# The opening of a perceiver layer: values over eight PSUM banks, row norms in pairs on two engines, keys projected ahead of queries

## The chip, the cores and the metric

The kernel runs on one core of one Trainium2 chip. A core has five engines with instruction streams of their own: TensorE (PE, matrix products into PSUM), VectorE (DVE), ScalarE (ACT), GpSimd (POOL) and SyncE (SP), which here only issues DMAs. They meet in semaphores. The metric is the device time of one execution in microseconds, the median of several runs.

## What is computed

One layer of three residual blocks over 512 rows of 1024 columns, in float32:

```python
x = x + cross_attention(layernorm(x), ctx)     # 16 heads of 64, causal
x = x + bitlinear_ffn(layernorm(x))            # weights rounded to -1, 0, 1, rows to int8
x = x + moe(layernorm(x))                      # 8 experts, top 2, and a shared one
# in the cross attention:
qp = q @ Wq.T                                  # q = layernorm(x): 512 x 1024
k, v = split(latent_kv @ Wkv_expand.T)         # latent_kv: 8192 x 256, of which the causal mask leaves 512 rows
out = softmax(mask(qh @ kh.T / 8)) @ vh
```

The change lies in the first 40 us: everything up to the exponentials of the first pair of heads. What follows is the same code.

## The kernel before

**Exact products.** To keep float32, each operand is split into a high part (a copy in a format that TensorE takes in full) and a low part (operand less high part), and `three` (L287) issues three matmuls for one product: high by high, high by low, low by high. So every operand needs a copy (as a rule ScalarE's) and a subtraction (VectorE's or GpSimd's).

**Loads.** SP issues in program order: the context `CTX` (two k-tiles of 128 by 512), the value weights in `RA[0]` (two k-tiles of 1024 columns, L387 and L388), the four tiles of rows `XRES`; then `qk_load(0)`, the query and key weights of head pair 0 (640 KB), also into `RA[0]` once `free_a[0]` says that it is read; four chunks of later weights into `RA[1]` to `RA[4]`; two more into `RX`; then `qk_load(1)` (L396), which waits until GpSimd has split the first. The chunks are only summed here (mean of absolute values, `absum` and `absum_x`); they share out between ScalarE (L1187, L1230) and VectorE (L684, L678).

**Values.** `values(n)` computes one 128 by 512 tile of V of four row tiles by two column halves, n = 2t + q, six matmuls each: for both k-tiles three. They go round four banks, `VB = (6, 7, 0, 1)`, so from the fifth on each waits for the evacuation of the one four before (`v_evac`, L1164). The first waits for both low parts of k-tile 0.

**Row norms.** `layer_norm_stats` (VectorE) takes the statistics of all four tiles (L359, L361), adds the constant, and waits for ScalarE's square root (`root`, L348), which stands in ScalarE's program behind four evacuations. `inv_sqrt` (L324 to L328) refines the reciprocal in five tiny instructions, each waiting for the one before; a sixth gives the offset. Four instructions (L667) write the normalised rows `XN`.

**Transposes.** `x_rows(t)` transposes a row tile in two halves through banks 2 to 5, ScalarE evacuates the high part (`xt_evac`, L1170), VectorE the low part (L672). Tiles 2 and 3 wait for the banks of 0 and 1. Two value tiles stand between them in TensorE's order.

**GpSimd** waits for all four `XN` and then splits the weights of pair 0 (`w_split`, L583 and L587, in two parts of 768 and 512 columns, high and low each).

**Projection.** `project_first(0)` takes the first half of the query product into bank 6 (12 matmuls), then the keys into bank 7 (6), `project_rest(0)` the other 12; `k_split` and `q_split` on ScalarE and VectorE split keys and queries; `scores`, row maxima (L702), exponentials (L1214) follow. From pair 1 on a loop does the same, with the attention of the pair before in between.

Of the kernel before, what the change touches and what calls it, by code (L numbers as in the profile page):

```python
# [21 lines left out]
P = 128  # L22
TOK, DM, LAT = 512, 1024, 256
NT = TOK // P
# [18 lines left out]
VB = (6, 7, 0, 1)  # L43
# [27 lines left out]
def program(nc, x, ctxT, wv, wqk, wo, wbit, n_gate, n_down, n_rms, wrt, wmoe, out, rows_dram):  # L71
    es = ExitStack()
    with es:
# [182 lines left out]
        for n in ("const", "v_eps", "sqrt", "ln",  # L256
                  "x_in0", "x_in1", "x_in2", "x_in3", "ctx_in", "norm_in",
                  "xn", "xt_pe", "xt_hi", "xt_lo", "ct_hi", "ct_lo", "wv_hi", "wv_lo", "v_pe", "v_ev", "wv_in",
# [93 lines left out]
        def layer_norm_stats(e):  # L352

            o = own["dve"]
            for t in range(NT):
                if veps[0] == 0:
                    e.wait_ge(s(f"x_in{t}"), 16)
                for h in range(2):
                    ins = e.bn_stats(BN[:, t, h, :], XRES[:, t, h * 512:h * 512 + 512])  # L359
                o(ins)  # L360
                o(e.bn_aggr(MV[:, t, :], BN[:, t, :, :].rearrange("p a b -> p (a b)")))  # L361
            e.tensor_scalar(col(2), MV[:, :, 1:2].rearrange("p a b -> p (a b)"), 1e-5, None, ALU.add)\
                .then_inc(s("v_eps"), 1)
            veps[0] += 1
            e.wait_ge(s("v_eps"), veps[0])
            inv_sqrt(e, col(2), col(3), col(0), veps[0])
            e.scalar_tensor_tensor(out=col(1), in0=MV[:, :, 0:1].rearrange("p a b -> p (a b)"), scalar=-1.0,
                                   in1=col(0), op0=ALU.mult, op1=ALU.mult).then_inc(s("ln"), 1)
# [182 lines left out]
        def _(e):  # L551
# [22 lines left out]
            def w_split(c, first, second=False):  # L574
                for q, at in enumerate((slice(0, WQA * P), slice(WQA * P, STRIP))):
# [4 lines left out]
                    if not first:  # L580
                        e.wait_ge(s(("k_pe", "q_pe")[q]), c)
# [13 lines left out]
            e.wait_ge(s("xn"), NT)  # L595
# [57 lines left out]
        def _(e):  # L653
# [3 lines left out]
            e.wait_ge(s("ct_hi"), 1)  # L657
            e.tensor_tensor(CTL[:, :, :], CTX[:, :, :], CTH[:, :, :].bitcast(f32), ALU.subtract)\
                .then_inc(s("ct_lo"), 1)
            for k in range(KL):  # L660
                e.wait_ge(s("wv_hi"), k + 1)
                e.tensor_tensor(WVL[:, k, :], RA[0][:, k * DM:k * DM + DM], WVH[:, k, :].bitcast(f32), ALU.subtract)\
                    .then_inc((s("wv_lo"), free_a[0])[k], 1)
            layer_norm_stats(e)
            e.wait_ge(s("ln"), 1)
            for t in range(NT):
                e.tensor_scalar(XN[t][:, :], XRES[:, t, :], col(0)[:, t:t + 1], col(1)[:, t:t + 1], ALU.mult, ALU.add)\  # L667
                    .then_inc(s("xn"), 1)
            for n in range(2 * NT):
                t, q = divmod(n, 2)  # L670
                e.wait_ge(s("xt_hi"), n + 1)
                e.tensor_tensor(XTL[:, 4 * q:4 * q + 4, t * P:t * P + P], r3(bank[2 + n % 4], 4),  # L672
                                XTH[:, 4 * q:4 * q + 4, t * P:t * P + P].bitcast(f32), ALU.subtract)\
                    .then_inc(s("xt_lo"), 1)
# [478 lines left out]
        def _(e):  # L1153
            e.preload_act_table(ACT.Sqrt)
            e.wait_ge(s("ctx_in"), 16)
# [17 lines left out]
            for n in range(4):  # L1173
                v_evac(n)
# [754 lines left out]
```

## Time and profile before

| | us |
|---|---|
| median of 3 runs | 683.06 (681.15 to 683.9) |
| profiled execution | 681.58 |
| its span | 680.0 |
| PE busy | 632.8 (93%) |
| DVE busy | 490.5 (72%) |
| ACT busy | 410.8 (60%) |
| POOL busy | 144.6 (21%) |
| mean granted TensorE clock | 0.987 of full |

The span runs from the first to the last instruction; 1.58 us lie around it. Matmuls are pipelined and each row's duration includes the way through the array, so a busy TensorE is not one at its peak: the distance between the starts of two rows tells the rate. In the page's chain that ended last TensorE has 61%, VectorE and ScalarE 15% each, and 6% is time in which an engine waited for nothing that the profile shows. In a timeline, "[1.99 <-issue]" behind a row is the idle time before it and what ended it. "(x36)" in a view by windows counts instructions.

### The profile page before, as it was taken

How to read it: one execution, taken by the hardware profiler on the slowest of the kernel's cores; microseconds unless marked ns; L12 is line 12 of the kernel's file. 1: busy time of each engine (PE TensorE's matmuls, PEld its weight loads, DVE VectorE, ACT ScalarE, POOL GpSimd, SP SyncE). 2: the span in 40 equal slices, each digit the busy share in tenths (PEclk: the TensorE clock that was granted, in tenths of full speed). 3: DMA queues.
4: the chain of work that ended last, by engine and by line, in shares of the span. 5: the costliest groups of instructions: out<-in, count | busy, mean ns of one | idle time of the engine just before them, and what ended most of it. 6: DMA issues, size and time to landing. Idle time of an engine off the chain costs nothing.

```text
span 680.0 us, 9662 instructions
## 1 busy us (share of the span) xinstructions
PE 632.8 (93%) x3275; PEld 475.9 (70%) x3289; DVE 490.5 (72%) x790; ACT 410.8 (60%) x531; POOL 144.6 (21%) x140
## 2 busy tenths in 40 slices
PE   4899999998999999749999999999999999999993
PEld 3778888886885444324467878787888778788772
DVE  5788887888786898688898366829192884564877
ACT  3778888888648898672574165527171771634740
POOL 1373445415000344219400400000000000000041
PEclk9999999999999999969999999999999999999997
DMA  8967776755167878709975619937466598292957
GB/s 332 384 241 294 300 291 240 314 236 192 52 278 282 337 293 357 302 0 363 409 294 232 267 67 380 406 137 301 173 238 256 193 380 349 104 362 70 387 174 265
DMA packets 30969, 179.02 MB, mean 263 GB/s; under 512 B 3808, under 2 KB 3808, under 8 KB 14688
## 3 DMA queue, kind: packets, MB, share of 16 engines
q1 hardware_dynamic: 25920, 161.39, 61.2%
q0 software_dynamic: 5024, 17.30, 6.7%
q8 instruction: 14, 0.23, 0.1%
q14 instruction: 11, 0.09, 0.0%
HBM read 155.62 MB, written 23.07 MB: 263 GB/s over the span
## 4 chain that ended last, share of the span: by engine, by line
PE 61%; DVE 15%; ACT 15%; issue 6%; DMA 2%; DVEq 0%; POOL 0%; ACTq 0%; SPq 0%
PE BK L293 13%; PE BK L299 13%; PE BK L294 13%; PE BK L287 9%; ACT PR L1214 4%; PE BK L1591 3%; ACT RA L1187 2%; PE BK L1691 2%; PE BK L1813 2%; DMA RD<-wbit 2%; PE BK L1576 1%; DVE BH L836 1%; ACT RA L1284 1%; PE BK L1745 1%; DVE HE L963 1%
## 5 line engine op out<-in xcount | busy, mean ns | idle before, releaser
L293 PE MATMUL BK<-WH,ETH 128*128 128x512 f32 x272 | 107.4, 395 | 1.5 <-ACT ETH L1435 1.4
L294 PE MATMUL BK<-WL,ETH 128*128 128x512 f32 x272 | 106.1, 390 | 0.0
L949 DVE TENSOR_TENSOR WL<-RA,WH 128x2048 fp32r<-128x2048 f32 x40 | 89.4, 2287 | 9.7 <-ACT WH L1402 9.5
L1402 ACT ACTIVATE WH<-RA 128x2048 fp32r<-128x2048 f32 x40 | 73.8, 1924 | 2.3 <-PE BK L1691 2.3
L1461 ACT ACTIVATE HTH<-BK 128x256 fp32r<-128x256 f32 x32 | 11.4, 383 | 95.2 <-PE BK L1813 95.1
L299 PE MATMUL BK<-WH,ETL 128*128 128x512 f32 x272 | 67.4, 390 | 0.0
L293 PEld LDWEIGHTS BK<-WH,ETH 128*128 128x128 f32 x272 | 51.0, 188 | 16.1 <-DVE WL L949 3.4
L647 POOL DMA_INDIRECT GA<-rows,SLOT x4 | 4.9, 1230 | 269.7 <-DVE WL L949 268.8
L299 PEld LDWEIGHTS BK<-WH,ETL 128*128 128x128 f32 x272 | 51.0, 188 | 10.6
L294 PEld LDWEIGHTS BK<-WL,ETH 128*128 128x128 f32 x272 | 51.1, 188 | 10.2
L963 DVE TENSOR_TENSOR HE<-BK,SI 128x256 f32<-128x256 f32 x34 | 12.9, 420 | 58.9 <-PE BK L299 58.1
L615 POOL TENSOR_TENSOR HB<-HB,ND (+2 forms) x28 | 31.1, 1127 | 111.5 <-DVE BH L836 110.7
L293 PE MATMUL BK<-WH,HTH 128*128 128x512 f32 x128 | 51.3, 401 | 0.6 <-ACT HTH L1461 0.6
L294 PE MATMUL BK<-WL,HTH 128*128 128x512 f32 x128 | 50.0, 391 | 0.0
L1284 ACT ACTIVATE RA<-RA,RT 128x2048 int16<-128x2048 f32 x22 | 43.8, 2001 | 5.3 <-DVE RT L765 3.1
L949 DVE TENSOR_TENSOR WL<-RC,WH 128x2048 fp32r<-128x2048 f32 x20 | 45.0, 2286 | 0.7 <-ACT WH L1402 0.7
L1645 PE MATMUL BK<-TG,XQ 128*128 128x512 bf16 x188 | 42.1, 379 | 0.3
L1402 ACT ACTIVATE WH<-RC 128x2048 fp32r<-128x2048 f32 x20 | 37.3, 1920 | 4.6 <-PE BK L299 4.6
L583 POOL TENSOR_TENSOR WQH<-RA,ONEF 128x768 fp32r<-128x768 f32 (+1 forms) x16 | 25.2, 1572 | 64.9 <-DMA RA<-wqk 46.5
L1691 PE MATMUL BK<-TD,HQT 128*128 128x512 bf16 x171 | 38.5, 381 | 0.3
L1214 ACT ACTIVATE PR<-BK,RT 128x512 f32<-128x512 f32 (+1 forms) x64 | 32.8, 536 | 7.6 <-DVE RT L702 7.4
L1187 ACT ACTIVATE RA<-RA 128x2048 f32<-128x2048 f32 x19 | 36.2, 1915 | 0.0
(252 smaller groups left out, 1400.5 us busy)
## 6 DMA issues: line engine op xcount, KB each, us to landing
RA<-wbit SPq DMA_DIRECT2D x53, 1024.0 KB, 6.5
RA<-wmoe SPq DMA_DIRECT2D x40, 1024.0 KB, 6.8
RC<-wmoe SPq DMA_DIRECT2D x20, 1024.0 KB, 7.7
rows<-ZERO POOLq DMA_DIRECT2D x34, 256.0 KB, 12.2
XG<-rows SPq DMA_DIRECT2D x15, 512.0 KB, 7.1
RD<-wbit SPq DMA_DIRECT2D x7, 1024.0 KB, 6.3
rows<-YS SPq DMA_DIRECT2D x14, 512.0 KB, 6.7
RA<-wqk SPq DMA_DIRECT2D x8, 640.0 KB, 7.4
```

The source lines that it names most:

```text
L287: m = e.matmul(dst, st, mv, start=first and i == 0 and j == 0, stop=last and i == n - 1 and j == 2)
L293: e.matmul(dst, sh, mh, start=first and i == 0, stop=False)
L294: e.matmul(dst, sh, ml, start=False, stop=False)
L299: m = e.matmul(dst, sl, mh, start=False, stop=i == len(pairs) - 1)
L615: e.tensor_tensor(HB[:, t, cs], HB[:, t, cs], ND[:, cs], ALU.mult).then_inc(s("hnd"), 1)
L949: e.tensor_tensor(WL[m][:, q * RAW:q * RAW + RAW], RC[j][:, :], WH[m][:, q * RAW:q * RAW + RAW].bitcast(f32), ALU.subtract)\
L1187: e.activation(RA[j][:, :], RA[j][:, :], ACT.Abs, accum_out=ACCW[:, column]).then_inc(free_a[j], 1)
L1214: ins = e.activation(PR[h][:, off:off + P * (i + 1)], STR[h][:, off:off + P * (i + 1)], ACT.Exp, bias=NM[:, h, i:i + 1], accum_out=RS[:, h ...
L1284: e.activation(RB16[j], RB[j][:, :], ACT.Copy, scale=SW[:, 0:1]).then_inc(s("rnd"), 1)
L1402: e.activation(WH[m][:, q * RAW:q * RAW + RAW], RC[2 * m + q][:, :], ACT.Copy)\
L1645: m = e.matmul(bank[out], XQ[:, k, t * P:t * P + P], weights[:, k, :], start=k == 0, stop=k == KD - 1)
L1691: m = e.matmul(bank[2 * (t % 2) + q], HQT[t % 2][:, k, :], (TD1[:, k, :] if k < 16 else TD2[:, k - 16, :])[:, q * 512:q * 512 + 512], star ...
```

## The change

- The context is loaded, copied and subtracted by k-tile: two DMAs, the second behind the first half of the value weights (five waits for DMAs in place of four). The value weights are copied by column half, the second k-tile's right half first.
- TensorE starts with k-tile 0 alone (`values_first`): for one column half the high by high products of all four row tiles, then low by high, then high by low. Each kind waits only for what it reads. The eight results lie in all eight banks. `values_rest` adds k-tile 1, right half first. No value matmul waits for an evacuation any more; the transposes wait for the four of the right half (banks 2 to 5).
- The low parts of the second k-tile of the value weights are made by GpSimd, which also frees `RA[0]`. GpSimd no longer waits for `XN`.
- Norms by pairs: statistics of tiles 0 and 1, constant, statistics of 2, scale of the pair, tile 0 normalised, statistics of 3, the second pair's. ScalarE normalises tiles 1 and 3 and takes two square roots, the first behind three evacuations, the second behind six. All low parts of transposed rows stand behind tile 2 on VectorE.
- TensorE transposes all four tiles behind the values; the keys of pair 0 are projected before the queries, and no longer wait for the transposed rows. GpSimd's split of pair 1 waits for `wq_pe`, the first half of the queries.
- `qk_load(1)` is issued ahead of the two loads into `RX`. Of the absolute sums one on ScalarE (`RX[0]`) and one on VectorE (`RX[1]`) stand behind the query split in place of ahead of it, and the key split comes earlier.

```diff
@@ sync
-            e.dma_start(CTX[:, :, :], ctxT).then_inc(s("ctx_in"), 16)
+            e.dma_start(CTX[:, 0, :], ctxT[:, 0, :]).then_inc(s("ctx_in"), 16)
             e.dma_start(RA[0][:, 0:DM], wv[:, 0:DM]).then_inc(s("wv_in"), 16)
+            e.dma_start(CTX[:, 1, :], ctxT[:, 1, :]).then_inc(s("ctx_in2"), 16)
...
+            qk_load(1)
             for j in range(2):
                 e.dma_start(RX[j][:, :], wbit[8 + j]).then_inc(in_x[j], 16)
-            qk_load(1)
@@ gpsimd
-            e.wait_ge(s("xn"), NT)
+            for n, q in enumerate((1, 0)):
+                cs = slice(q * 512, q * 512 + 512)
+                e.wait_ge(s("wv_hi"), n + 3)
+                e.wait_ge(s("wv_lo"), 2)
+                e.tensor_tensor(WVL[:, 1, cs], RA[0][:, DM + q * 512:DM + q * 512 + 512], WVH[:, 1, cs].bitcast(f32),
+                                ALU.subtract).then_inc((s("wv_lp"), free_a[0])[n], 1)
             w_split(0, True)
@@ vector
-            layer_norm_stats(e)
-            e.wait_ge(s("ln"), 1)
-            for t in range(NT):
+            def row_norm(t):
+                e.wait_ge(s("ln"), t // 2 + 1)
                 e.tensor_scalar(XN[t][:, :], XRES[:, t, :], col(0)[:, t:t + 1], col(1)[:, t:t + 1], ALU.mult, ALU.add)\
                     .then_inc(s("xn"), 1)
...
+            row_stats(e, 0)
+            row_stats(e, 1)
+            row_variance(e, 0)
+            row_stats(e, 2)
+            row_scale(e, 0)
+            row_norm(0)
+            row_stats(e, 3)
+            row_variance(e, 2)
+            row_scale(e, 2)
+            row_norm(2)
+            rows_t_lo(0)
+            rows_t_lo(1)
+            rows_t_lo(2)
+            rows_t_lo(3)
...
             absum(2, slice(5, 6), 16)
+            k_split(0)
             absum(4, slice(7, 8), 16)
-            k_split(0)
+            q_split(0)
             absum_x(1, 9)
-            q_split(0)
@@ scalar
-            for n in range(4):
+            for n in range(3):
                 v_evac(n)
-            root(e, col(2), col(3))
+            root(e, col(2)[:, 0:2], col(3)[:, 0:2])
+            v_evac(3)
+            row_norm(1)
             v_evac(4)
             v_evac(5)
-            xt_evac(0)
-            xt_evac(1)
+            root(e, col(2)[:, 2:4], col(3)[:, 2:4])
             v_evac(6)
             v_evac(7)
+            xt_evac(0)
+            row_norm(3)
+            xt_evac(1)
             xt_evac(2)
             xt_evac(3)
...
+            k_split(0)
             absum(1, slice(4, 5), 16)
             absum(3, slice(6, 7), 16)
+            q_split(0)
             e.wait_ge(in_x[0], 16)
             e.activation(RX[0][:, :], RX[0][:, :], ACT.Abs, accum_out=ACCW[:, 8:9]).then_inc(sum_x[0], 1)
-            k_split(0)
-            q_split(0)
@@ tensor
+            def values_first(q):
+                cs = slice(q * 512, q * 512 + 512)
+                for n, (A, B) in enumerate(((CTH, WVH), (CTL, WVH), (CTH, WVL))):
+                    e.wait_ge(*((s("wv_hi"), q + 1), (s("ct_lo"), 1), (s("wv_lo"), q + 1))[n])
+                    for t in range(NT):
+                        e.matmul(bank[VB[q][t]], A[:, 0, t * P:t * P + P], B[:, 0, cs], start=n == 0, stop=False)
...
-            for n in range(6):
-                values(n)
-            e.wait_ge(s("const"), 15)
-            x_rows(0)
-            x_rows(1)
-            values(6)
-            values(7)
-            x_rows(2)
-            x_rows(3)
+            values_first(0)
+            values_first(1)
+            e.wait_ge(s("ct_lo"), 2)
+            e.wait_ge(s("wv_lp"), 1)
+            values_rest(1)
+            e.wait_ge(free_a[0], 1)
+            values_rest(0)
+            e.wait_ge(s("const"), 15)
+            e.wait_ge(s("v_ev"), NT)
+            for t in range(NT):
+                x_rows(t)
             e.wait_ge(s("v_ev"), 2 * NT)
-            e.wait_ge(s("xt_lo"), 2 * NT)
...
+                if isinstance(c, int) and c == 0:
+                    three(e, bank[7], part(range(KL), CTH, CTL, 4), True, True).then_inc(s("k_pe"), 1)
+                    e.wait_ge(s("xt_lo"), 2 * NT)
+                m = three(e, bank[6], part(range(4), XTH, XTL, 0), True, False)
```

## Rows read from the trace of the kernel before

**Rows 1.** Stages: from:to, length, busy PE PEld DVE ACT POOL, clock, DMA, GB/s
```profile
9.50:20.00 10.50, 10.47 (x36) 8.04 (x36) 8.92 (x21) 3.08 (x6) 0.00 (x0) 1.00 1.01 415
```

**Rows 2.** Timeline of ScalarE's opening: start, length, line, operation, out<-in
```profile
7.06 1.06 ACT L1159 ACTIVATE WVH<-RA 128x1024 fp32r<-128x1024 f32 x1 [1.89 <-DMA RA<-wv]
17.80 0.20 ACT L348 ACTIVATE SM<-SM 128x4 f32<-128x4 f32 x1
```

**Rows 3.** Timeline of TensorE, the first and the tenth matmul
```profile
9.52 0.76 PE L287 MATMUL BK<-WVH,CTH 128*128 128x512 f32 x1 [9.52 <-DVE WVL L662]
13.49 0.59 PE L287 MATMUL BK<-WVH,CTH 128*128 128x512 f32 x1
```

**Rows 4.** Timeline of TensorE, first and last of the 30 matmuls of projection 0
```profile
28.71 0.47 PE L287 MATMUL BK<-XTH,WQH 128*128 128x512 f32 x1 [1.99 <-issue]
35.37 0.39 PE L287 MATMUL BK<-XTH,WQL 128*128 128x512 f32 x1
```

**Rows 5.** Timeline of VectorE: statistics, root, normalised rows, low parts
```profile
15.27 1.29 DVE L359 BATCH_NORM_STATS2 BN<-XRES 128x6 f32<-128x512 f32 x2
18.10 0.18 DVE L324 RECIPROCAL SM<-SM 128x4 f32<-128x4 f32 x1 [1.09 <-ACT SM L348]
19.31 2.98 DVE L667 TENSOR_SCALAR XN<-XRES,SM 128x1024 f32<-128x1024 f32 x4
26.12 2.48 DVE L672 TENSOR_TENSOR XTL<-BK,XTH 128x512 fp32r<-128x512 f32 x4 [1.44 <-ACT XTH L1170]
```

**Rows 6.** Timeline of VectorE and ScalarE, end of the opening
```profile
34.35 2.28 DVE L678 TENSOR_REDUCE ACCW<-RX 128x1 f32<-128x2048 f32 x1
36.54 0.68 DVE L693 SCALAR_TENSOR_TENSOR QL<-BK,QH 128x512 fp32r<-128x512 f32 x1
31.19 1.94 ACT L1230 ACTIVATE RX<-RX 128x2048 f32<-128x2048 f32 x1
35.79 0.60 ACT L1203 ACTIVATE QH<-BK 128x512 fp32r<-128x512 f32 x1 [2.08 <-PE BK L287]
36.92 1.28 ACT L1235 ACT_TABLE_LOAD   x1
39.01 0.69 ACT L1214 ACTIVATE PR<-BK,RT 128x512 f32<-128x512 f32 x1 [0.81 <-DVE RT L702]
```

**Rows 7.** SP issue and landing of query weights, GpSimd split
```profile
10.70 0.33 SPq L396 DMA_DIRECT2D RA<-wqk  x1
RA<-wqk SPq DMA_DIRECT2D x1, 640.0 KB, 4.3
22.38 1.86 POOL L583 TENSOR_TENSOR WQH<-RA,ONEF 128x768 fp32r<-128x768 f32 x1 [18.40 <-DVE XN L667]
24.31 1.83 POOL L587 TENSOR_TENSOR WQL<-RA,WQH 128x768 fp32r<-128x768 f32 x1
27.46 1.28 POOL L587 TENSOR_TENSOR WQL<-RA,WQH 128x512 fp32r<-128x512 f32 x1
```

**Rows 8.** Timeline of VectorE alone and beside GpSimd
```profile
149.51 2.29 DVE L731 TENSOR_TENSOR WOL<-RA,WOH 128x2048 fp32r<-128x2048 f32 x1 [1.11 <-ACT WOH L1240]
151.36 4.88 POOL L605 TENSOR_TENSOR WOL<-RA,WOH 128x2048 fp32r<-128x2048 f32 x1 [14.03 <-ACT WOH L1240]
155.58 0.17 DVE L710 RECIPROCAL RT<-RT 128x4 f32<-128x4 f32 x1
160.13 4.61 POOL L605 TENSOR_TENSOR WOL<-RA,WOH 128x2048 fp32r<-128x2048 f32 x1
163.72 3.17 DVE L731 TENSOR_TENSOR WOL<-RA,WOH 128x2048 fp32r<-128x2048 f32 x1
```

**Rows 9.** Timeline of GpSimd and VectorE where both have work queued
```profile
240.28 1.71 POOL L615 TENSOR_TENSOR HB<-HB,ND  x1
240.79 1.76 DVE L808 TENSOR_SCALAR TX<-RA 128x2048 bf16<-128x2048 int16 x1
```

**Rows 10.** Busy time by stage, the columns of rows 1, behind the last matmul
```profile
670.00:675.00 5.00, 0.00 (x0) 0.00 (x0) 4.89 (x6) 0.00 (x0) 0.00 (x0) 0.77 0.62 254
```

More of the change, by code:

```diff
@@ L350, in program, with row_stats, row_variance, row_scale @@
         veps = [0]
-        def layer_norm_stats(e):
+        def row_stats(e, t):
             o = own["dve"]
-            for t in range(NT):
[L356 to L362, printed above, removed]
+            e.wait_ge(s(f"x_in{t}"), 16)
+            for h in range(2):
+                ins = e.bn_stats(BN[:, t, h, :], XRES[:, t, h * 512:h * 512 + 512])
+            o(ins)
+            o(e.bn_aggr(MV[:, t, :], BN[:, t, :, :].rearrange("p a b -> p (a b)")))
+        def row_variance(e, t):
+            e.tensor_scalar(col(2)[:, t:t + 2], MV[:, t:t + 2, 1:2].rearrange("p a b -> p (a b)"), 1e-5, None, ALU.add)\
                 .then_inc(s("v_eps"), 1)
             veps[0] += 1
[L365 to L368, printed above, removed]
+        def row_scale(e, t):
+            two = slice(t, t + 2)
+            inv_sqrt(e, col(2)[:, two], col(3)[:, two], col(0)[:, two], veps[0])
+            e.scalar_tensor_tensor(out=col(1)[:, two], in0=MV[:, two, 0:1].rearrange("p a b -> p (a b)"), scalar=-1.0,
+                                   in1=col(0)[:, two], op0=ALU.mult, op1=ALU.mult).then_inc(s("ln"), 1)
         def tile_stats(e, t, eps):
@@ L580, in w_split @@
                     if not first:
-                        e.wait_ge(s(("k_pe", "q_pe")[q]), c)
+                        e.wait_ge(s(("wq_pe" if second else "k_pe", "q_pe")[q]), c)
                     hi, lo = (T[:, :, :].rearrange("p a b -> p (a b)")[:, at] for T in (WQH, WQL))
@@ L656, in _ @@
             e.sem_inc(s("h"), 8)
[L657 to L663, printed above, removed]
-            layer_norm_stats(e)
@@ L667, in _, with rows_t_lo @@
+            context_lo(1)
+            def row_norm(t):
+                e.wait_ge(s("ln"), t // 2 + 1)
                 e.tensor_scalar(XN[t][:, :], XRES[:, t, :], col(0)[:, t:t + 1], col(1)[:, t:t + 1], ALU.mult, ALU.add)\
                     .then_inc(s("xn"), 1)
[L669 to L674, printed above, removed]
+            def rows_t_lo(t):
+                for q in range(2):
+                    n = 2 * t + q
+                    e.wait_ge(s("xt_hi"), n + 1)
+                    e.tensor_tensor(XTL[:, 4 * q:4 * q + 4, t * P:t * P + P], r3(bank[2 + n % 4], 4),
+                                    XTH[:, 4 * q:4 * q + 4, t * P:t * P + P].bitcast(f32), ALU.subtract)\
+                        .then_inc(s("xt_lo"), 1)
@@ L1542, in project_first @@
                 e.wait_ge(s("wq_a"), c + 1)
-                three(e, bank[6], part(range(4), XTH, XTL, 0), True, False)
-                e.wait_ge(s("ot_lo"), c if not isinstance(c, int) or c else 1)
+                if isinstance(c, int) and c == 0:
+                    three(e, bank[7], part(range(KL), CTH, CTL, 4), True, True).then_inc(s("k_pe"), 1)
+                    e.wait_ge(s("xt_lo"), 2 * NT)
+                m = three(e, bank[6], part(range(4), XTH, XTL, 0), True, False)
+                if isinstance(c, int) and c == 0:
+                    m.then_inc(s("wq_pe"), 1)
+                    return
+                e.wait_ge(s("ot_lo"), c)
                 three(e, bank[7], part(range(KL), CTH, CTL, 4), True, True).then_inc(s("k_pe"), 1)
```

66 lines of the change are left out of this document (40 added, 26 removed).

## The prediction

> **What bounds the kernel now.** I read the page first, whose chain that ended last is mostly TensorE's; but that is an average over stages, and the change touches nothing behind the first head pair. So next came the busy time by stages: from 9.5 to 20 TensorE is busy for 10.47 of 10.50 us, and the DMA engines are full at 415 GB/s [rows 1]. Both are misleading, which only the third view shows, the timeline of the opening engine by engine: the chain passes from engine to engine, and these are its stations. ScalarE's high part of the first value weights starts when the DMA lands at 7.06 [rows 2]; TensorE begins at 9.52 [rows 3], because VectorE makes the low part first. Its first ten matmuls are 0.44 us apart, which for 512 columns is the 1.2 GHz level (the granted clock of that stretch stands at 1.00 in [rows 1], so here the steps tell it), and the later ones 0.23 (28.71 to 35.37 is 29 steps [rows 4]), the 2.4 GHz level; before 9.52 it had done nothing. The square root of the row norms is at 17.80, since ScalarE takes it behind four evacuations [rows 2]; VectorE starts on it at 18.10, normalises from 19.31 to 22.29 and ends the low parts of the transposed rows at 28.60 [rows 5]. Then thirty projection matmuls run from 28.71 to 35.76 [rows 4]. The low queries start at 36.54, behind the last 2.28 us reduction, and the exponentials, after the first row maxima, at 39.01 [rows 6]. That last number is what I carry: from it on both kernels do the same work in the same order, pair after pair, with nothing I can find that would give time back.
>
> **The change, part by part, in order of time.**
>
> *First matmul.* Ahead of the value weights lies half a context (262 KB less, 0.63 us at 415 GB/s [rows 1]), so they land near 6.4 (bounds 5.9 to 7.06, if the smaller pieces bring nothing). The first high part is half as wide: the row of 1.06 for 1024 columns [rows 2] and 0.60 for 512 [rows 6] say 0.6. No low part is needed for the first four matmuls. TensorE starts near 7.1, 2.4 us early. The context splits lie in the waits for DMAs and cost nothing; if the DMAs came no earlier they would still be ahead of the weights.
>
> *Values.* Still 48 matmuls. Ten at 0.44 last to 11.5. The third finished bank is now the 33rd matmul (24 first parts, 3 for each bank), 22 steps of 0.23 later: it ends at 16.9. Before, the fourth bank ended at 17.3. So of the 2.4 us only 0.4 reach the square root: ScalarE evacuates the third bank (0.5) and takes the root at 17.4; VectorE has it at 17.7. The statistics of rows 0 to 2 (1.3 a tile and the aggregate, 15.27 [rows 5]) are done by 14.5 and wait.
>
> *GpSimd.* It now makes the low parts of the second value weights, 1.28 each of 512 columns [rows 7], 9.0 to 11.6, and these free the weight buffer; so the SP queue, which waits for it, issues the first query weights at 11.6 and not 10.70 [rows 7]. These landed 4.3 us after issue [rows 7]; with the older rows drained by then I take 15.5 (15.0 to 15.9). Before, GpSimd waited for the four normalisations and split them from 22.38 to 28.74, 6.36 us [rows 7]. That wait is gone: it splits from 15.5 to about 22. Nobody needs the result before the projection.
>
> *The collision.* Now the split lies upon the row norms. What rows show: a subtraction of VectorE with two SBUF inputs took 2.29 alone and 3.17 from 163.72 on, while GpSimd was busy until 164.74; a reciprocal took 0.17 in the middle of a GpSimd instruction [rows 8]. And where GpSimd has instructions queued the two alternate: GpSimd's row from 240.28 is 1.71 long and ends at 241.99, VectorE's from 240.79 ends 0.56 behind that [rows 9]. So an instruction of VectorE waits for the whole of GpSimd's, gets its turn, and its successor waits for the whole of GpSimd's next. Behind the root stand a reciprocal, three tensor-tensor forms, one scalar form, and one combination that reads two SBUF operands, all on two columns and each waiting for the one before (0.2 a step, 18.10 to 19.31 [rows 5]). No row shows such tiny instructions beside GpSimd, so their cost lies between nothing and one GpSimd instruction each. I take the full wait, because the rows above are blocked to the end of GpSimd's instruction whatever their own length. Then: multiplication asked at 17.9, granted at 19.3 (1.86 and 1.83 of split gone [rows 7]); the next behind the third instruction at 20.7; the next behind the fourth at 22.15; the norm's scale is ready at 22.7, against 18.9 without the collision. The Trainium skill has a rule for this (SBUF — State Buffer, section "Who interferes with whom"): a VectorE instruction with two SBUF inputs, or in a two-port mode, and a GpSimd instruction that reads SBUF exclude each other for the whole instruction. The trace agrees for large ones, 3.17 against 2.29; it states no exception for small ones.
>
> *Second pair of rows.* Row 0 is normalised at 23.5 (0.75 each [rows 5]), the statistics of row 3 follow to 25.1, ScalarE meanwhile does row 1 (1.06) and two evacuations, root at 25.25, scale ready at 26.7, row 2 at 27.5. The low parts of the transposed rows now wait behind all this. ScalarE puts its own row 3 (1.06) ahead of the second row's evacuations, so these low parts run without a gap only from the third on: 29.1 + 6 × 0.62 = 32.85 (0.62 each [rows 5]), against 28.60. Taking two of the four normalisations from VectorE (1.5 us) is paid with a second root and a second chain of six (1.5).
>
> *Projection.* The six key matmuls now run in the wait, 30.9 to 32.3; 24 instead of 30 lie behind the rows, which brings 1.4. Queries end at 32.9 + 23 × 0.23 + 0.39 = 38.6 (35.76 before).
>
> *Absolute sums.* One of VectorE (2.28) and one of ScalarE (1.9) move behind the query splits. They are no longer in front of anything that is late, but they are in front of the row maxima and of the table load. High queries at 38.6, low at 39.2, maxima at 42.0; ScalarE: 38.6 + 0.5 + 1.9 + 0.6 + 1.28 = 42.9 [rows 6]. Exponentials start at 42.9 and not 39.01: +3.9. Their data: the two loads now stand behind the second query weights, issued at 22; with four loads of 1 MB issued from 12 on and 0.65 MB ahead of them, at 415 GB/s they land by 32, needed at 39.
>
> *Clock.* TensorE ends the values at 20.3 and waits for row 0 until 23.5. The level held through 1.99 us of idleness at 28.7 [rows 4], and near the end, in a stretch without a matmul from 670 on, the granted clock has a mean of 0.77 over five microseconds, so it stood at 1 for some 2.7 and at half for the rest [rows 10]. So 3.2 us may lose it. Keys and the first queries then run at 0.44: 0 to 1.4 us. I take 0.6.
>
> Sum: +3.9 + 0.6 = +4.5. On the profiled execution's own 681.58 that is 686.1. It lies 1.5 below the median of 683.06, to which I apply the same difference: 687.6.
>
> **Rivals.**
> *Small instructions are not blocked* (not slower). The scale is then ready at 18.9; only the normalisation of row 0 waits 0.5 for GpSimd. Low parts end near 29.5, queries at 35.2 (0.6 early, for the keys are out of the way), low queries at 35.8, maxima at 38.6, ScalarE 35.2 + 4.3 = 39.5. With the moved sums that is +0.5: 683.5, range 682 to 685. It decides at the first tiny instruction behind the root. For it: the reciprocal of [rows 8]. Against it: that one reads a single operand.
> *The clock falls and stays down* through keys and queries: 30 × 0.21 = 6.3 at most, of which the keys hide some; with the collision +9, 691 to 692. Against it: at the start ten matmuls brought the clock up [rows 3].
> *The opening simply works*: weights at 5.9, no blocking, the root not late. Then the queries end at 34.3, exponentials near 38.4: 682.4. It can't be more, since the maxima stand behind three reductions and two splits of VectorE (7.9 us) after the last low part, wherever they are put.
> *The identity function of the row norms needs another table than the root*: 1.28 [rows 6] each way, 2.6 to 5 us more. The copies around the root reloaded nothing, so I hold it small, inside the upper range. The Trainium skill says (ScalarE: Activation LUTs, "Table sets: the hidden batching unit") that identity is in every set; by it the cost is nothing, and no row here shows the function.
>
> **How the numbers follow.** Collision with the clock kept or lost briefly 0.54 (685.9 to 689.5); small instructions free 0.34; opening works 0.04; clock down or tables 0.08. A measurement of this kernel can tell about 0.5%, 3.4 us, from no change; the boundary of slower is 686.5. Of the first case 0.44 lies above it, of the last all: slower 0.52, same 0.45, faster 0.03. Range 682.6 to 690.5, leaving out a tenth on each side. The likeliest case's own is 685.9 to 689.5.
>
> **What would show it.** VectorE's small rows near 17.9 to 22 of over 1 us each (right) or 0.16 (the rival). First matmul near 7.1; root near 17.4; GpSimd's split from 15.5; last low part near 32.9 (rival 29.5); key matmuls wholly before it; a spacing of 0.44 in keys and queries if the clock fell; first exponential at 42.9 against 39.5; and the distance from it to the end as before, 641.0. The prediction is wrong if the query weights land after the norms are done, for then nothing collides, or if the later stages take the delay back.

## The result and the profile after

The changed kernel takes 686.51 us (median of 7 runs, 684.64 to 688.14) beside 683.44 for the kernel before on the same chip (7 runs, 681.15 to 684.4). The ratio is 1.005, with a 95% interval of 1.0032 to 1.0068, so it is slower by 2.2 to 4.6 us. The profiled execution took 686.51, with a span of 684.8 and a mean clock of 0.982 (681.58, 680.0 and 0.987 before).

These are the stations of the opening, in us from the span's start. The second column is read or worked out from the rows ahead of the prediction, the last from the rows below.

| station | before | forecast | after |
|---|---|---|---|
| first matmul | 9.52 | 7.1 | 6.53 |
| first query weights issued | 10.70 | 11.6 | 12.86 |
| GpSimd's split begins | 22.38 | 15.5 | 18.11 |
| (first) root | 17.80 | 17.4 | 17.46 |
| row 0: normalisation asked | 19.31 | 22.7 | 23.10 |
| row 0 normalised | 20.1 | 23.5 | 24.94 |
| second root | none | 25.25 | 26.62 |
| last low part of the transposed rows ends | 28.60 | 32.85 | 34.10 |
| first exponential | 39.01 | 42.9 | 44.25 |
| from it to the end of the span | 641.0 | 641.0 | 640.55 |

**Where the time goes** is in VectorE's timeline of the changed kernel (start, length, then as in [rows 5]). The six tiny instructions behind the root stand one below the other; in the kernel before they took 0.2 a step from 18.10 to 19.31.

```profile
17.76 0.17 DVE L324 RECIPROCAL SM<-SM 128x2 f32<-128x2 f32 x1 [2.03 <-ACT SM L348]
17.95 0.16 DVE L325 TENSOR_TENSOR SM<-SM 128x2 f32<-128x2 f32 x1
18.15 1.82 DVE L326 TENSOR_TENSOR SM<-SM 128x2 f32<-128x2 f32 x1
20.00 0.17 DVE L327 TENSOR_SCALAR SM<-SM 128x2 f32<-128x2 f32 x1
20.20 1.64 DVE L328 TENSOR_TENSOR SM<-SM 128x2 f32<-128x2 f32 x1
21.88 1.18 DVE L371 SCALAR_TENSOR_TENSOR SM<-MV,SM 128x2 f32<-128x2 f32 x1
23.10 1.84 DVE L681 TENSOR_SCALAR XN<-XRES,SM 128x1024 f32<-128x1024 f32 x1
...
28.05 0.81 DVE L681 TENSOR_SCALAR XN<-XRES,SM 128x1024 f32<-128x1024 f32 x1
...
30.42 3.68 DVE L688 TENSOR_TENSOR XTL<-BK,XTH 128x512 fp32r<-128x512 f32 x6 [0.36 <-ACT XTH L1215]
```

And GpSimd's timeline of the same stretch:

```profile
10.31 2.52 POOL L604 TENSOR_TENSOR WVL<-RA,WVH 128x512 fp32r<-128x512 f32 x2 [6.34 <-ACT WVH L1192]
18.11 1.83 POOL L588 TENSOR_TENSOR WQH<-RA,ONEF 128x768 fp32r<-128x768 f32 x1 [5.28 <-DMA RA<-wqk]
20.02 1.80 POOL L592 TENSOR_TENSOR WQL<-RA,WQH 128x768 fp32r<-128x768 f32 x1
21.79 1.25 POOL L588 TENSOR_TENSOR WQH<-RA,ONEF 128x512 fp32r<-128x512 f32 x1
23.13 1.27 POOL L592 TENSOR_TENSOR WQL<-RA,WQH 128x512 fp32r<-128x512 f32 x1
```

Add start and length on both sides. VectorE's tiny row from 18.15 ends at 19.97, GpSimd's from 18.11 at 19.94. VectorE's from 20.20 ends at 21.84, GpSimd's from 20.02 at 21.82; VectorE's from 21.88 at 23.06, GpSimd's from 21.79 at 23.04. Three times an instruction on two columns ends 0.02 or 0.03 behind the GpSimd instruction during which it was asked. The row from 17.95 was asked before GpSimd had begun and took 0.16. The three cost 1.66, 1.48 and 1.02 us above their own length, 4.2 together. The normalisation of row 0 (0.81 alone, at 28.05) took 1.84, 1.0 more, and ended 0.54 behind GpSimd's fourth.

The second chain of six, 26.86 to 28.01, took 0.2 a step. GpSimd was done by then.

How the split came to lie there: SP's issue in the timeline, the transfer in the view of DMAs from 12 to 20 (size, us to landing), and ScalarE's timeline.

```profile
12.86 0.33 SPq L401 DMA_DIRECT2D RA<-wqk  x1
```

```profile
RA<-wqk SPq DMA_DIRECT2D x1, 640.0 KB, 5.2
```

```profile
5.85 1.15 ACT L1192 ACTIVATE WVH<-RA 128x512 fp32r<-128x512 f32 x2 [1.53 <-DMA RA<-wv]
...
9.60 1.15 ACT L1192 ACTIVATE WVH<-RA 128x512 fp32r<-128x512 f32 x2 [1.19 <-DMA RA<-wv]
...
17.46 0.20 ACT L348 ACTIVATE SM<-SM 128x2 f32<-128x2 f32 x1
...
26.62 0.20 ACT L348 ACTIVATE SM<-SM 128x2 f32<-128x2 f32 x1 [1.31 <-DVE SM L363]
...
42.96 1.28 ACT L1284 ACT_TABLE_LOAD   x1
44.25 0.69 ACT L1263 ACTIVATE PR<-BK,RT 128x512 f32<-128x512 f32 x1
```

The second k-tile of the value weights was there at 9.60, so GpSimd's low parts ended at 12.83. The query weights were issued at once and landed at 18.1, 0.3 behind the start of VectorE's chain. This moment is not fixed: in the eight traces with these opening loads (this one and e1, e3 to e6, e8, e9, below) the query weights were issued between 11.83 and 13.21 and landed between 15.4 (e9) and 18.4 (e5).

**TensorE** of the changed kernel: its first matmuls, the first transposes, and the key product; then the busy time by stage (columns of [rows 1]).

```profile
6.53 2.08 PE L1555 MATMUL BK<-WVH,CTH 128*128 128x512 f32 x4 [6.53 <-ACT WVH L1192]
...
25.09 3.65 PE L1570 MATMUL BK<-IDF,XN 128*128 128x128 f32 x16 [4.76 <-DVE XN L681]
...
32.18 0.48 PE L287 MATMUL BK<-CTH,WQH 128*128 128x512 f32 x1
32.49 0.39 PE L287 MATMUL BK<-CTL,WQH 128*128 128x512 f32 x1
32.72 0.39 PE L287 MATMUL BK<-CTH,WQL 128*128 128x512 f32 x1
```

```profile
20.00:24.00 4.00, 0.33 (x2) 0.00 (x0) 3.90 (x4) 0.90 (x1) 3.90 (x3) 0.80 1.01 426
24.00:28.00 4.00, 2.91 (x14) 2.94 (x15) 3.49 (x11) 2.69 (x7) 0.40 (x1) 0.50 0.99 386
...
32.00:36.00 4.00, 3.66 (x18) 2.74 (x17) 4.00 (x5) 3.20 (x4) 0.00 (x0) 1.00 0.19 74
```

It started 3.0 us earlier than before, finished the values and then stood for 4.76 us. The granted clock fell to 0.50, and the transposes ran at the lower level. By the keys it was back (steps of 0.23).

### The profile page after: what moved, and what is told of

Same layout as the page of the kernel before. It is cut to its first block, busy times and chain, and to the rows that moved or that the text cites. A ratio compares the mean times of both kernels' runs of the same rounds, so it can differ in the third digit from the quotient of the medians.

```text
span 684.8 us, 9676 instructions
## 1 busy us (share of the span) xinstructions
PE 635.9 (93%) x3275; PEld 477.7 (70%) x3289; DVE 494.3 (72%) x796; ACT 413.4 (60%) x537; POOL 147.1 (21%) x142
## 3 DMA queue, kind: packets, MB, share of 16 engines
q0 software_dynamic: 5024, 17.30, 6.6%
## 4 chain that ended last, share of the span: by engine, by line
PE 61%; DVE 15%; ACT 15%; issue 4%; DMA 3%; DVEq 0%; POOL 0%; SPq 0%; ACTq 0%
PE BK L293 14%; PE BK L294 13%; PE BK L299 13%; PE BK L287 8%; ACT PR L1263 5%; ACT RA L1236 3%; PE BK L1646 2%; PE BK L1746 2%; PE BK L1868 2%; PE BK L1631 1%; DMA RA<-wbit 1%; PE BK L1555 1%; DVE BH L866 1%; ACT RA L1333 1%; ACT PTH L1270 1%
```

## The experiments

The theory: GpSimd's split lies on the norms' chain of tiny instructions, and each of these waits for a whole GpSimd instruction. The rivals: the late root and the two chains are the cost, or the moved sums are, or the load order, or the clock. All experiments were run beside the kernel before; its median was 683.18 for e1 to e4, 683.33 for e5 to e9, 682.84 for e10 and e11.

**e1: the split waits for VectorE's two normalisations again.**

```diff
+            e.wait_ge(s("xn"), 2)
             w_split(0, True)
             w_split(1, False, True)
```

> The changed kernel, but GpSimd again waits before its split of pair 0, now for the two tiles that VectorE normalises. Theory of the collision: the instructions of 1.82, 1.64, 1.18 and 1.84 us behind the first root fall to 0.16 and 0.8, the scale of the first pair is ready near 19 in place of 23.1, the last low part of the transposed rows ends near 29 in place of 34.1, and the first exponential starts at 39.5 to 40.5 in place of 44.25 (the two loads for the moved sums now come later, near 37, and may cost the rest); time about 4 us under the changed kernel, level with the kernel before within 0.3%. Rival, the order of VectorE's own work (a second root, a second chain of tiny instructions, all low parts behind tile 2) is what costs: the tiny instructions get short, but the first exponential stays at 42 or later and the time over 685.

Measured: 685.9, ratio 1.0041 (1.0024 to 1.0057). The timelines of e1, VectorE and TensorE, and one stage:

```profile
17.89 0.16 DVE L326 TENSOR_TENSOR SM<-SM 128x2 f32<-128x2 f32 x1
...
18.68 0.81 DVE L682 TENSOR_SCALAR XN<-XRES,SM 128x1024 f32<-128x1024 f32 x1
...
38.70 2.29 DVE L709 TENSOR_REDUCE ACCW<-RX 128x1 f32<-128x2048 f32 x1 [2.38 <-DMA RX<-wbit]
```

```profile
45.62 4.00 PE L1632 MATMUL BK<-IDF,PR 128*128 128x128 f32 x20 [2.74 <-DVE PR L745]
```

```profile
46.00:48.00 2.00, 2.00 (x11) 2.00 (x10) 1.88 (x6) 0.29 (x1) 0.00 (x0) 0.50 0.99 401
```

The chain is free: every tiny row has its 0.16 or 0.17, row 0 is asked at 18.68 and not 23.10, and the last low part ends at 29.10 and not 34.10. So the collision is there and the split causes it. But of these 5.0 us only 2.6 reach the first exponential (41.62), and almost nothing the median: 685.9 is what the rival asked for, while the rows are those of the theory. The row from 38.70 says why: a sum waits 2.38 us for its DMA. The change had also put `qk_load(1)` ahead of the two `RX` loads in SP's queue. `qk_load(1)` waits for GpSimd's split, which now ends near 30; it is issued at 29.85 and `RX` at 30.22 (24.42 and 24.79 in the changed kernel, where nothing waited for them). The maxima stand behind that sum. In addition TensorE stood for 2.74 us ahead of the transposes of the first pair's probabilities, the clock fell to 0.50, and the distance from the first pair's exponentials to the second pair's was 17.4 instead of 16.5.

**e2: the kernel before, with the wait of GpSimd for `XN` removed.**

```diff
-            e.wait_ge(s("xn"), NT)
             w_split(0, True)
```

> The kernel before, with only GpSimd's wait for the four normalised tiles taken out, so that it splits as soon as the weights have landed (near 15). Theory of the collision: three or four of the tiny instructions behind the root take 1.2 to 1.8 us, the first tile is normalised near 22 in place of 19.3, the first exponential starts near 41.4 in place of 39.0, time +2.4 us (+0.35%). Rival, that the two engines do not exclude each other for tiny operands and the long rows of the changed kernel are waits for something else: nothing moves, within 0.1%.

Measured: 687.36, ratio 1.0066 (1.0043 to 1.009): one removed line makes the old kernel slower, by the ratio 4.5 us (2.9 to 6.1). GpSimd, VectorE and TensorE of e2:

```profile
17.16 1.85 POOL L587 TENSOR_TENSOR WQL<-RA,WQH 128x768 fp32r<-128x768 f32 x1
18.96 1.29 POOL L583 TENSOR_TENSOR WQH<-RA,ONEF 128x512 fp32r<-128x512 f32 x1
20.33 1.27 POOL L587 TENSOR_TENSOR WQL<-RA,WQH 128x512 fp32r<-128x512 f32 x1
```

```profile
19.06 1.22 DVE L326 TENSOR_TENSOR SM<-SM 128x4 f32<-128x4 f32 x1
...
20.51 1.10 DVE L328 TENSOR_TENSOR SM<-SM 128x4 f32<-128x4 f32 x1
...
21.85 2.98 DVE L666 TENSOR_SCALAR XN<-XRES,SM 128x1024 f32<-128x1024 f32 x4
```

```profile
31.27 0.46 PE L287 MATMUL BK<-XTH,WQH 128*128 128x512 f32 x1 [1.99 <-issue]
...
31.93 0.63 PE L287 MATMUL BK<-XTH,WQL 128*128 128x512 f32 x1
```

The two blocked rows end at 20.28 and 21.61, 0.03 and 0.01 behind GpSimd's. The query weights landed earlier here, at 15.2, so less of the split lies on the chain. A third row, from 18.73, took 0.30 and ends at 19.03, 0.02 behind GpSimd's. The normalisation is asked 2.5 us late (21.85 against 19.31), 2.1 of it the chain and 0.4 a later root. That is the delay that I expected, though I had expected three or four rows over 1 us. But the first exponential is 4.15 late, at 43.16, not 2.4. The other 1.6 are the clock: the same 1.99 us of idleness as in [rows 4] ended this time in steps of 0.43 (31.93, 32.35, 32.78 and on to 34.49), and only from 34.91 on in 0.23. I had not expected that.

**e3: the changed kernel with the sums in their old places, ahead of the query splits.**

```diff
 (VectorE)
-            q_split(0)
             absum_x(1, 9)
+            q_split(0)
 (ScalarE)
-            q_split(0)
             e.wait_ge(in_x[0], 16)
             e.activation(RX[0][:, :], RX[0][:, :], ACT.Abs, ...)
+            q_split(0)
```

> The changed kernel, but with the two absolute sums ahead of the query split again on ScalarE and on VectorE. Theory of the prediction (the sums behind the split stand in front of the first exponential, the time ahead of it is idle on both engines by 1.5 and 1.7 us): ScalarE's high queries 0.3 later, VectorE's low queries 0.7 later, first exponential 0.5 earlier, at 43.7; time -0.5 us, which can be read in the trace and not in the medians. Rival, that the sums in front delay the scores by their full length: first exponential at 45 or later.

Measured: 686.34, ratio 1.0046 (1.003 to 1.0063), the same as the changed kernel. The first exponential is at 43.52, 0.73 sooner. The norms were 0.46 earlier by themselves (row 0 was asked at 22.64), but the last sixteen transposes still ran at the lower clock level (0.50 from 28 to 32, against 0.84), and by the end of the last low part only 0.14 of that lead was left (33.96 against 34.10). So 0.59 comes from the place of the sums, where I had expected 0.5; e4 and e8 below give the same. VectorE's chain of e3, however, shows a form that the changed kernel didn't show blocked:

```profile
18.04 1.25 DVE L325 TENSOR_TENSOR SM<-SM 128x2 f32<-128x2 f32 x1
...
19.52 1.68 DVE L327 TENSOR_SCALAR SM<-SM 128x2 f32<-128x2 f32 x1
```

The instruction with one tensor operand (L327) waits too, and which of the six are caught differs from one execution to the next.

**e8 and e4: the wait and the old order of loads; and with the sums ahead as well.** e8 is e1 with this, e4 is e8 with the edit of e3.

```diff
-            qk_load(1)
             for j in range(2):
                 e.dma_start(RX[j][:, :], wbit[8 + j]).then_inc(in_x[j], 16)
+            qk_load(1)
```

> The changed kernel with GpSimd's wait and with the two loads for the moved sums ahead of the second query weights, but the two sums still behind the query split. It stands between the run with the wait alone (first exponential 41.6, which waited 2.4 us for such a load) and the one with all three (38.1). Theory: the load costs 2.2 of these 3.5, the sums' place 1.2: first exponential at 39.3 to 39.5. Rivals: 38.1 (the place of the sums costs nothing) or 41.6 (the load was not it). No clock lost in the first pair's transposes, so that pair's period is 16.7 and not 17.4; time 1.2 us over the run with all three.

> The changed kernel with GpSimd's wait, the two sums ahead of the query split, and their two loads ahead of the second query weights: what is left of the change is the values over eight banks, the norms by pairs and the keys ahead of the queries. Theory: last low part near 29, last query matmul near 34.9 (35.76 before), low queries near 36.9, first exponential at 38.7 (39.0 before); time within 0.2% of the kernel before, some 4.5 us under the changed one. Rival, that the order of the norms costs by itself: first exponential at 40.5 or later.

Measured: e8 682.7, ratio 0.9983 (0.9966 to 1.0001); e4 682.34, 0.9987 (0.9971 to 1.0002). ScalarE's first exponential of e8, and of e4:

```profile
38.77 0.69 ACT L1264 ACTIVATE PR<-BK,RT 128x512 f32<-128x512 f32 x1
```

```profile
38.12 0.69 ACT L1264 ACTIVATE PR<-BK,RT 128x512 f32<-128x512 f32 x1 [0.86 <-DVE RT L733]
```

This is the main finding. With the collision and what hangs on it gone, the changed kernel's first exponential moves from 44.25 to 38.77, and by the ratios it gains 0.67%, 4.6 us. What is left of the change in e8 stands 0.24 ahead of the kernel before at this station and is not to be told from it by time. (In e4 VectorE took the low queries at 35.65, where I had expected 36.9, since the sum ahead of them began sooner.) Against e1, the order of the loads is worth 2.85 there, once the split is late (expected: 2.2). The sums behind the splits cost 0.65 at the first exponential (expected: 1.2) and 0.4 at the second pair's, and nothing that the times show.

One interval sorts the runs better than the single station. From the end of the last low part to the first exponential it is 10.41 in the kernel before, 10.15 where VectorE's sum stands behind the query split (the changed kernel, e5, e8, e11) and 9.56 or 9.57 where it stands ahead (e3, e4, e9, e10). Only where something else came in between was it longer: the late load in e1, the clock in e2, both in e6. So the place of the sum costs 0.59 each time, and everything ahead of the last low part passes through to the first exponential one for one. At that part e8 and e4 stand at 28.62 and 28.55, the kernel before at 28.60 (29.18 and 28.88 in e10 and e11, with the same code up to it): TensorE's start, 3 us earlier, and the norms by pairs have together brought at most 0.6 there.

**e5: the root ahead of the first evacuations, no wait.** In the changed kernel the variance of rows 0 and 1 is ready at 14.30, and ScalarE takes the root at 17.46, behind three evacuations.

```diff
-            for n in range(3):
-                v_evac(n)
             root(e, col(2)[:, 0:2], col(3)[:, 0:2])
-            v_evac(3)
+            for n in range(4):
+                v_evac(n)
```

> The changed kernel with ScalarE's first square root ahead of the evacuations instead of behind three of them; no wait of GpSimd's added. Theory (ports, and a root that is late although its input is ready at 14.3): the scale of the first pair is ready near 17.1, before GpSimd's split begins at 17.5 to 18, tile 0 is normalised near 17.9; now the second chain lies beside the split and has the rows of over 1 us, so the last low part ends near 31 in place of 34.1 and the first exponential is at 41 to 41.5 in place of 44.25; time 2 to 3 us under the changed kernel. Rival (only the first chain matters, the second is short): first exponential at 39.5.

Measured: 684.63, ratio 1.001 (0.9997 to 1.0022). The first chain now runs before the split, 16.12 to 17.30. The second falls into it; GpSimd's four rows start at 18.52, 20.43, 22.20 and 23.54. VectorE of e5:

```profile
19.59 0.79 DVE L363 TENSOR_SCALAR SM<-MV 128x2 f32<-128x2 f32 x1
...
20.85 1.40 DVE L325 TENSOR_TENSOR SM<-SM 128x2 f32<-128x2 f32 x1
22.29 1.19 DVE L326 TENSOR_TENSOR SM<-SM 128x2 f32<-128x2 f32 x1
...
23.71 1.10 DVE L328 TENSOR_TENSOR SM<-SM 128x2 f32<-128x2 f32 x1
```

The collision moves with the chain; it belongs to the overlap in time, not to an instruction. It costs 3.8 here, nearly what it cost on the first chain, and the first exponential comes at 41.76, 2.5 earlier, because rows 0 and 1 are normalised 5.8 us earlier (17.30 against 23.10) and only the second pair is late. By the ratios that is 2.7 us under the changed kernel, as expected.

**e6: e4 and e5 together.**

> The run with GpSimd's wait, sums ahead and loads ahead, and the first root ahead of the evacuations too. Theory: scale of the first pair near 17, last low part near 28.0 (28.55 there), first exponential near 37.6 (38.12 there, 39.01 before): the root was 1.2 us late, but ScalarE's place for the second root gives half of it back. Time 0 to 1 us under that run, faster than the kernel before by 0.15 to 0.3%. Rival: nothing gained, since the second pair of rows sets the end: first exponential at 38.1.

Measured: 682.21, ratio 0.9986 (0.997 to 1.0003), no better than e4, though the last low part ends a microsecond earlier (27.56 against 28.55). TensorE's scores of e6 and the stage:

```profile
35.81 0.70 PE L1619 MATMUL BK<-KH,QH 64*128 64x512 f32 x2 [2.02 <-DVE QL L724]
```

```profile
36.00:39.00 3.00, 3.00 (x22) 2.72 (x22) 0.80 (x2) 1.27 (x3) 2.92 (x3) 0.50 1.02 431
```

The queries are done sooner, but VectorE takes the low query part behind its third sum, which waited 0.33 for its load, at 35.07. So TensorE stands for 2.02 us, the clock falls, the scores run at the lower level, and the first exponential is at 38.12 as in e4. In e9, below, the scores also start at 35.81, at the upper level, and the exponential is 0.6 earlier. The next pair then comes 17.4 later and not 16.7.

**e9: norms, evacuations and table load in another order.** e8 with VectorE's sum ahead of the split (ScalarE's behind it), and ScalarE's opening changed as follows:

```diff
-            for n in range(3):
-                v_evac(n)
             root(e, col(2)[:, 0:2], col(3)[:, 0:2])
-            v_evac(3)
+            for n in range(4):
+                v_evac(n)
             row_norm(1)
+            root(e, col(2)[:, 2:4], col(3)[:, 2:4])
             v_evac(4)
             v_evac(5)
-            root(e, col(2)[:, 2:4], col(3)[:, 2:4])
-            v_evac(6)
-            v_evac(7)
-            xt_evac(0)
             row_norm(3)
+            xt_evac(0)
             xt_evac(1)
+            v_evac(6)
+            v_evac(7)
             xt_evac(2)
             xt_evac(3)
+            e.preload_act_table(ACT.Exp)
...
             values_hi(0)
-            e.preload_act_table(ACT.Exp)
```

> A version meant to beat both: GpSimd's wait; both roots as early as their inputs allow; ScalarE's rows 3 ahead of the evacuations of transposed rows and of the last values; the loads ahead; VectorE's sum ahead of the query split, ScalarE's behind; the exponential's table loaded right after the last transposed rows instead of ahead of the first exponential. Theory: last low part near 27.3, last query matmul ends near 33, first exponential near 37.0 (39.01 before, 44.25 changed), bound by VectorE's three sums and two splits; time about 2 us under the kernel before (-0.3%). Rival: VectorE's work is already the bound of the run with all three, and it stays at 38.

Measured: 681.55, ratio 0.9974 (0.996 to 0.9988), so it beats both kernels, the one before by 0.8 to 2.7 us. The first exponential was expected at 37.0 and came at 37.54. VectorE and ScalarE of e9:

```profile
25.50 2.48 DVE L689 TENSOR_TENSOR XTL<-BK,XTH 128x512 fp32r<-128x512 f32 x4 [0.44 <-ACT XTH L1216]
...
35.08 0.68 DVE L724 SCALAR_TENSOR_TENSOR QL<-BK,QH 128x512 fp32r<-128x512 f32 x1
```

```profile
26.95 1.28 ACT L1233 ACT_TABLE_LOAD   x1
...
37.54 0.69 ACT L1264 ACTIVATE PR<-BK,RT 128x512 f32<-128x512 f32 x1 [0.68 <-DVE RT L733]
```

The table load sits in a gap of ScalarE. The first root is at 13.30, rows 0 and 2 are normalised from 15.92 and 20.82, and the first exponential is 1.5 ahead of the kernel before. The clock stood at 1.00 in every stage from 20 to 36. What bounds it now is VectorE: from the last low part (27.98) three sums and two splits run without a gap to 35.76. The prediction had that as the reason why no opening could bring much. Which of its parts made e9 faster isn't shown: the early root is in e6 too, which brought nothing over e4, and e6's last low part ends even sooner (27.56). Behind it e6 lost the 0.33 for the load and 0.6 by the clock, and e9 neither. Nor do the times tell e9 from e4 and e6, whose intervals overlap with its own.

**e10 and e11: the kernel before with the keys projected first; and with one sum of each engine behind the query split as well.** The central part of the diff:

```diff
-            e.wait_ge(s("xt_lo"), 2 * NT)
...
-                three(e, bank[6], part(range(4), XTH, XTL, 0), True, False)
-                e.wait_ge(s("ot_lo"), c if not isinstance(c, int) or c else 1)
+                if isinstance(c, int) and c == 0:
+                    three(e, bank[7], part(range(KL), CTH, CTL, 4), True, True).then_inc(s("k_pe"), 1)
+                    e.wait_ge(s("xt_lo"), 2 * NT)
+                m = three(e, bank[6], part(range(4), XTH, XTL, 0), True, False)
```

> One part alone: the kernel before, with only the keys of pair 0 projected ahead of the queries and split as soon as they are there; the sums stay ahead of the query split. Theory (VectorE's three sums and two splits, 7.9 us behind the last low part, bound the end): the last query matmul ends 1.4 us earlier, at 34.4, but the low queries stay at 36.5 and the first exponential at 39.0; time unchanged. Rival, the six matmuls were on the path: first exponential at 37.8, time -1.3 us.

> The same with one sum of each engine moved behind the query split as in the changed kernel. Theory: low queries at 35.0, but then 2.2 us of sum in front of the row maxima and 1.9 in front of ScalarE's table load: ScalarE 34.4 + 0.5 + 1.9 + 0.6 + 1.28 = 38.7, first exponential at 38.7 to 39.0, time within 0.5 us of the kernel before. Rival, the sums out of the way bring the 1.4 us through: 37.6.

Measured: e10 682.34, ratio 0.9989 (0.9973 to 1.0005); e11 682.05, 0.999 (0.9977 to 1.0003). First exponentials at 38.74 and 39.03. By time this part of the change can't be told from nothing. The high queries come earlier (35.03 and 34.71 against 35.79), but in e10 VectorE reaches the low part only at 36.28, and in e11 the sum stands in front of the maxima. The stations alone understate it, since the root came 0.57 and 0.28 later in these two than in the kernel before: counted from the last low part, e10 is 0.85 shorter and e11 0.26. Most of the 0.85 is VectorE's wait of 0.75 for the high keys ahead of 33.74 in the kernel before, which is gone in e10.

## Why the prediction was right, and where its sizes were off

Direction, mechanism and range held. The forecast was +4.5 us. The medians say +3.1 (2.2 to 4.6), the profiled executions +4.9.

*The collision* is right, and it was the term with no row behind it. The value that I took, a whole GpSimd instruction for each of three tiny ones, measured 4.2 where the sum had 3.8. The rival in which small instructions aren't blocked is excluded by the rows from 18.15 on, and by e1, e2, e5 and e8. The Trainium skill's rule (SBUF — State Buffer, section "Who interferes with whom"), the exclusive lock for the whole instruction, holds here down to 128x2. It counts TENSOR_SCALAR among the forms that can take the shared pair when their operands allow it, and e3's 1.68 agrees.

*The landing of the query weights* is the term that was mis-sized most. I had them issued at 11.6 and there at 15.5; they were issued at 12.86, took 5.2 us and were there at 18.1. The second k-tile of the value weights could be copied only from 9.60, against 8.36 for ScalarE's second copy in the kernel before, and no term stood for that. In two of the eight traces with these loads (e4 and e9) the weights landed at 15.7 and 15.4, as forecast, so part of this is scatter.

*The normalisation of row 0* follows from it. By the forecast's own times GpSimd is done at about 22, before row 0 is asked at 22.7, so the 0.75 of [rows 5] stood there with reason. With the split 2.6 us later GpSimd had its fourth instruction left (23.13 to 24.40), and row 0 took 1.84, 1.0 more than alone. With the 0.4 by which the scale was later it makes up the 1.35 us by which the first exponential missed the forecast (44.25 against 42.9). All stations from row 0 on are 1.2 to 1.4 behind, so the intervals between them were right.

*Luck* had a part in the sum. The 1.0 that was missing for row 0 and the 0.6 for the clock, which cost nothing, have opposite signs (the 42.9 in the table is without the 0.6). And the first chain was caught only because the weights landed in time: it began at 17.76, would have ended at 18.95 if free, and the split began at 18.11. Had they come a microsecond later, the second chain would probably have been caught in its place, as in e5; the prediction's condition for "nothing collides" should have named both chains. The rest of the opening was close: first matmul at 6.53, 0.6 sooner than forecast, root at 17.46 against 17.4.

*The clock* fell as feared, from 1.00 to 0.50 (24 to 28), and cost about nothing where I had 0.6. The transposes ran at half speed, but ScalarE evacuated the first of them only at 27.69, behind the second root and two value tiles, when row 0's had been done for some 0.8 us, and the keys found the clock back at its upper level. e1, e2 and e6 show what it costs where nothing covers it: 0.9 (e1), 1.6 (e2) and 0.6 (e6).

*Tables*: there is no table load around the second root and the two normalisations on ScalarE, so identity brings none. The Trainium skill's page (ScalarE: Activation LUTs, "Table sets: the hidden batching unit"), which has identity in every set, agrees.

*The sums* behind the query splits, in front of the row maxima and the table load, were part of ScalarE's 42.9 and had no price of their own. The runs give one, 0.59 from the last low part to the first exponential (e3 against the changed kernel, e4 against e8, e10 against e11); it is not to be seen in the times.

*The distance to the end* was 640.55 against 641.0. It isn't constant from run to run: among these kernels, whose code behind 60 us is the same, it ranges from 640.5 to 643.5. Of that 0.9 (e1) and 0.7 (e6) lie in the first pair; from the second pair's exponentials on the intervals between the eight pairs agree in all kernels within 0.04. Most of the rest is one place in the stage of the experts. Here it is in the kernel before and in e8 (columns of [rows 1]):

```profile
405.00:410.00 5.00, 3.59 (x19) 2.85 (x17) 4.75 (x6) 5.00 (x6) 0.00 (x0) 1.00 0.62 216
405.00:410.00 5.00, 3.69 (x9) 2.97 (x10) 5.00 (x5) 4.30 (x4) 0.00 (x0) 0.66 0.74 261
```

The granted clock falls there in e8, and ScalarE's rows of e8, 0.8 ahead of the kernel before's at 404.02 (404.83 there), are 0.9 behind at 413.68 (412.76 there). It does so in e1, e3, e5, e8 and e9, at a price of 1.6 to 1.7 us each, and these are the five with the longest distances but for e6's. Without it and the losses in the first pair all twelve lie between 640.5 and 641.8. All five have the changed opening and none of the four built on the kernel before loses the clock there; with one trace of each it isn't shown whether that is chance. That is why two profiled executions are compared at the first exponential, and kernels by medians. At that station the traces show a gap of 5.2 where the medians show 3.1. Part of it is that the root of the kernel before stood at 17.80 in its profile and at 18.08 to 18.37 in e2, e10 and e11, whose code up to it is the same, while the changed kernel's norms stood 0.46 behind e3's. The rest I can't place.

**What stays open** is, first, what decides whether an idle stretch loses the clock. 1.99 us kept it in the kernel before; in e2 2.41 us ahead of the first transposes kept it (16 transposes in 1.94) and 1.99 lost it later; 2.02 lost it in e6, 2.33 in e4 and e8 (16 transposes in 3.59, hidden as in the changed kernel). The length of the gap alone doesn't decide. And the pieces of the change that speed up TensorE's opening weren't tried one by one; together with the rest of the change, and with the collision away, they are worth 1.2 (e8) and 0.9 us (e4) by the ratios against the kernel before, and both intervals include nothing.

## What to carry to other kernels

An early start for a helper engine is not free because nobody needs its result: before a wait on GpSimd is removed, lay its instructions over VectorE's timeline and look for chains of tiny dependent instructions, since each of them can cost a whole GpSimd instruction, and five or six stand in every norm. A wait that looks superfluous may be the only thing that keeps two engines apart, and a DMA queue ordered around an early split goes wrong when the split is made late again (e1), so the two are changed together. Time won by TensorE at the start is worth little while the next station is set by another engine's program order: its 3.0 us at the first matmul, together with the norms by pairs, were at most 0.6 at the last low part (e8 and e4).

## What the runs showed of the hardware that I had not expected

- Tiny VectorE instructions (128x2 and 128x4) with two SBUF operands, and a TENSOR_SCALAR with one, took up to 1.8 us where they met GpSimd's queued instructions, against 0.16: each ran to 0.01 to 0.03 behind the GpSimd instruction beside it. The RECIPROCAL was never caught (0.17 or 0.18), though GpSimd was at work in e2, e3 and e5 when it was asked (18.51, 17.84, 20.65). TENSOR_REDUCE and the statistics beside GpSimd kept their length too (2.28 from 41.17 in the changed kernel, 1.28 from 18.03 in e5).
- Who is caught is a matter of hundredths of a microsecond: the row from 20.00 slipped in between two GpSimd instructions (19.94 to 20.02) in 0.17, and the same instruction took 1.68 in e3.
- About 2 us of idleness can lose TensorE's upper level (1.99 in e2, 2.02 in e6), which cost 0.9 to 1.6 us where nothing lay over it; the same length kept it in [rows 4]. What decides is open. In the stage of the experts a fall cost 1.6 to 1.7 us.
- Loads split into smaller pieces brought the first value weights sooner in all eight traces that have them (ScalarE copies them from 5.67 to 6.09, against 6.81 to 7.06 in the four others) and the last ones no sooner or later, with far more scatter (8.56 to 9.92, against 8.11 to 8.54).
